# A cross-attention and expert kernel on one core: the gated bias in one product, the front's loads and clears laid out anew

## The reference, cut to what matters

```python
# x, ctx: (8, 256, 128)
n = layernorm(x)
q, k, v = heads(n @ W_Q.T), heads(ctx @ W_K.T), heads(ctx @ W_V.T)     # 8 heads of 16
attn = softmax(q @ k.T / 4, axis=heads)                                # over the heads
x = x + (attn @ v) @ W_O.T
n = layernorm(x)
logits = n @ Wr + br                                                   # 8 experts, best 2 kept
gates = softmax(where(top2, logits, -inf))
h = relu(n @ W1[e] + b1[e])                                            # 128 -> 256, each expert
x = x + sum_e gates[e] * (h @ W2[e]) + gates @ b2
```

## Time and profile before

| | |
|---|---|
| median of 3 runs | 209.75 us (209.21 to 209.9) |
| span of the profiled execution | 207.8 us, from its first instruction to its last |
| PE busy (matmuls) | 199.5 us, 96% |
| DVE / ACT / POOL busy | 167.8 / 132.2 / 112.3 us |
| instructions | 4986 |

### The profile page before, as it was taken

One profiled execution on the slowest core, in us unless ns is written; L12 is line 12 of the kernel. 1 busy time (PEld: TensorE's weight loads), 2 busy tenths in 40 slices (PEclk: granted clock), 3 DMA queues, 4 the chain that ended last, 5 costly groups with the idle time before them and its releaser, 6 DMA issues.

```text
span 207.8 us, 4986 instructions
## 1 busy us (share of the span) xinstructions
PE 199.5 (96%) x1752; PEld 176.5 (85%) x1752; DVE 167.8 (81%) x453; ACT 132.2 (64%) x316; POOL 112.3 (54%) x132
## 2 busy tenths in 40 slices
PE   6999988798999999999999999999999999999995
PEld 6845976686799979997999799998998899789994
DVE  6398769889789999899788988898999888556633
ACT  2236748697568847797677767677757776345441
POOL 8502647869976378629561966376746674010000
PEclk9999999999999999999999999999999999999999
DMA  6649595716515133423140504241000000000000
GB/s 175 160 127 286 153 279 148 224 46 183 158 62 145 69 108 106 103 76 104 41 147 25 170 3 151 57 144 36 0 0 28 0 2 3 25 3 2 25 3 25
DMA packets 20264, 18.70 MB, mean 90 GB/s; under 512 B 1776, under 2 KB 18704, under 8 KB 20240
## 3 DMA queue, kind: packets, MB, share of 16 engines
q1 hardware_dynamic: 17344, 16.85, 28.0%
q10 hardware_dynamic: 2896, 1.54, 2.8%
HBM read 11.83 MB, written 6.55 MB: 88 GB/s over the span
## 4 chain that ended last, share of the span: by engine, by line
PE 91%; DVE 3%; ACT 2%; issue 1%; POOL 1%; POOLq 0%; ACTq 0%; DVEq 0%
PE y_ps L436 28%; PE h_ps L421 22%; PE score_ps L361 7%; PE misc_ps L380 6%; PE score_ps L349 6%; PE h_ps L369 4%; PE score_ps L277 3%; PE misc_ps L401 2%; PE score_ps L338 2%; PE score_ps L421 2%; PE misc_ps L389 2%; PE misc_ps L287 1%; PE misc_ps L327 1%; PE misc_ps L306 1%; PE misc_ps L300 1%
## 5 line engine op out<-in xcount | busy, mean ns | idle before, releaser
L695 ACT ACTIVATE hT<-h_ps,b_sb 128x256 f32<-128x256 f32 x118 | 49.4, 470 | 33.3 <-PE h_ps L421 32.1
L436 PE MATMUL y_ps<-w_sb,hT 128*128 128x128 f32 x508 | 68.0, 277 | 0.0
L436 PEld LDWEIGHTS y_ps<-w_sb,hT 128*128 128x128 f32 x508 | 62.8, 191 | 3.5 <-issue 2.2
L1188 POOL TENSOR_TENSOR half_sum<-e_sb 128x512 f32<-128x512 f32 x28 | 37.3, 1332 | 30.8 <-ACT e_sb L667 30.5
L938 DVE TENSOR_TENSOR attn<-e_sb,e_rcp 128x1024 f32<-128x1024 f32 x32 | 42.1, 1319 | 3.3 <-ACT e_rcp L678 3.3
L930 DVE TENSOR_REDUCE shift_m<-score_ps 128x128 fp32r<-128x1024 f32 x32 | 38.7, 1212 | 2.2 <-PE score_ps L338 1.1
L421 PE MATMUL h_ps<-x1T_hi,w_lo 128*128 128x256 f32 x118 | 37.7, 320 | 1.5 <-ACT hT L695 0.9
L667 ACT ACTIVATE e_sb<-score_ps 128x1024 f32<-128x1024 f32 x32 | 32.8, 1024 | 5.6 <-PE score_ps L361 5.4
L1007 DVE SCALAR_TENSOR_TENSOR acc<-y_ps,gates,acc 128x128 f32<-128x128 f32 x96 | 29.0, 342 | 8.6 <-PE y_ps L436 7.3
L421 PE MATMUL h_ps<-x1T_hi,w_hi 128*128 128x256 f32 x118 | 33.1, 280 | 0.0
L421 PE MATMUL h_ps<-x1T_lo,w_hi 128*128 128x256 f32 x118 | 33.1, 280 | 0.0
(11 more groups left out here) (117 smaller groups left out, 291.3 us busy)
## 6 DMA issues: line engine op xcount, KB each, us to landing
k_scratch<-k_parts SPq DMA_DIRECT2D x14, 256.0 KB, 2.6
k_stack<-k_scratch SPq DMA_DIRECT2D x14, 256.0 KB, 4.0
q_stack<-q_scratch SPq DMA_DIRECT2D x28, 128.0 KB, 2.7
q_scratch<-q_parts SPq DMA_DIRECT2D x7, 256.0 KB, 2.7
w_sb<-in_w SPq DMA_DIRECT2D x1, 1024.0 KB, 6.6
out_y<-y_out SPq DMA_DIRECT2D x7, 128.0 KB, 1.9
x_all<-in_x ACTq DMA_DIRECT2D x1, 768.0 KB, 6.2
ctxT<-in_ctx_t SPq DMA_DIRECT2D x1, 640.0 KB, 6.1
```

The source lines that it names most:

```text
L436: mm = nc.tensor.matmul(product(j, t), hT[:, j % 2, c, t * P:(t + 1) * P], w2_sb[:, e * HC + c, :], start=(c == 0), stop=(c == HC - 1))
L695: op = nc.scalar.activation(hT[:, j % 2, c, :], hidden(j)[:, c * S:(c + 1) * S], ACT.Relu, bias=b1_sb[:, e * HC + c:e * HC + c + 1])
L1188: nc.gpsimd.tensor_tensor(half_sum[:], e[:, 0:HQ // 2], e[:, HQ // 2:HQ], ALU.add).then_inc(sum_step, 1)
```

## The change

It does these things; the orders on the engines are otherwise as before.

- The gated bias becomes two products of 128 x 128 weights by 128 columns in the rounded fp32r format. `b2_sb` is loaded as 16 stacked copies; `split_b2` on DVE makes from it the rows `b2_rows` (high part for most rows, low part for others). `transpose_gates` first writes the high part of the gates twice and their low part once into `gate_parts` (two more DVE instructions for each sample). `block_gates`, new on POOL, multiplies the transposed gates by `group_of`, so that `gatesD` is block diagonal. `gated_b2` now waits for `gates_blocked`, which POOL raises.
- `split_b2(0)` stands on DVE between `head_max(1, 1)` and `ln1(5 * TT, NT, 4)`; `block_gates(0)` and `block_gates(1)` on POOL behind `head_sum(2, 1)` and `head_sum(3, 1)`, and in `period` behind `head_sum(now, 1)`.
- The rows of sample 0 are loaded in two halves, first on each queue; the attention weights are second on ACT's queue; all other early loads go to SP's queue. b2 is one load in place of four, so the small loads count 64 and not 112.
- `neg_ident` is made by ACT. POOL's clears are cut in parts and stand behind `ln1_rstd_of` of sample 0 (`v_pad` of sample 0, gates, iota) and of sample 1 (the rest).
- `keep_warm(12)` is `keep_warm(8)`; the later `keep_warm` and both `fill` are gone.
- `expert_up(b, 0)` makes the four products with x1T_hi first and waits for x1T_lo only then.

```diff
             def gated_b2(b, freed, n):
                 if b == 0:
-                    pe.wait_ge(small_in, 112)
+                    pe.wait_ge(b2_rows_made, 1)
                 wait(pe, freed, n)
-                pe.wait_ge(gatesT_made, b + 1)
+                pe.wait_ge(gates_blocked, b + 1)
                 for t in range(TT):
-                    for g in range(P // 32):
-                        rows = slice(32 * g, 32 * g + E)
-                        mm = nc.tensor.matmul(misc_ps[32 * g:32 * g + 32, t * P:(t + 1) * P], gatesT[rows, t, :],
-                                              b2_sb[rows, :], start=True, stop=True)
+                    mm = nc.tensor.matmul(misc_ps[:, t * P:(t + 1) * P], gatesD[:, t, :, :].rearrange("p g k -> p (g k)"),
+                                          b2_rows[:], start=True, stop=True)
                 mm.then_inc(b2_done, 1)
...
                 if e == 0:
-                    pe.wait_ge(x1T_lo_made, b + 1)
+                    pe.wait_ge(x1T_hi_made, b + 1)
...
+                if e == 0:
+                    passes = [(c, w, x1T_hi) for c in range(HC) for w in (w1_lo, w1_hi)] + [(c, w1_hi, x1T_lo) for c in range(HC)]
...
+                    if e == 0 and k == 2 * HC:
+                        pe.wait_ge(x1T_lo_made, b + 1)
...
             def beginning():
                 project_k(0, None, 0)
                 project_v(0, None, 0)
-                keep_warm(5)
                 transpose_xn(0, None, 0)
-                keep_warm(1)
                 project_q(0, xnT_taken, 1)
                 project_k(1, k_first_made, 1)
-                keep_warm(2)
...
-                fill(4)
                 scores(1, 0)
...
-                fill(4)
                 transpose_x1n(0, v_taken, 3)
...
             def take_v(b):
                 wait(act, av_done, b - 3)
-                if b == 0:
-                    act.wait_ge(v_zeroed, 1)
+                if b < 4:
+                    act.wait_ge(v_zeroed, b + 1)
...
+            act.dma_start(x_all[:, 1, :], x_rows[:, 1, :]).then_inc(x0_in, 16)
             act.dma_start(w_qkvo[:], w_attn).then_inc(wq_in, 16)
             nc.scalar.preload_act_table_set("natural_log_exp_and_others")
...
+            act.wait_ge(ident_made, 1)
+            nc.scalar.activation(neg_ident[:], ident[:], ACT.Copy, scale=-1.0).then_inc(neg_ident_made, 1)
...
+            def split_b2(b):
+                dve.wait_ge(neg_ident_made, 1)
+                nc.vector.tensor_reduce(neg_lo_row[:], neg_ident[:].bitcast(F32).rearrange("p (g r) -> p g r", r=32)[:, :, 16:24],
+                                        AX.XY, ALU.min)
+                nc.vector.tensor_reduce(group_of[:], ident[:].rearrange("p (g r) -> p g r", r=32), AX.X,
+                                        ALU.max).then_inc(b2_step, 1)
+                dve.wait_ge(small_in, 64)
+                nc.vector.tensor_copy(b2_hi[:], b2_sb[:]).then_inc(b2_step, 1)
+                dve.wait_ge(b2_step, 2)
+                nc.vector.scalar_tensor_tensor(out=b2_rows[:], in0=b2_hi[:].bitcast(F32), scalar=neg_lo_row[:, 0:1], in1=b2_sb[:],
+                                               op0=ALU.mult, op1=ALU.add).then_inc(b2_rows_made, 1)
...
             def transpose_gates(b):
                 dve.wait_ge(gates_made, b + 1)
...
+                nc.vector.tensor_copy(gate_parts[:].rearrange("p t (k s) -> p t k s", s=2 * E)[:, :, :, 0:E],
+                                      gates[:, b % 2].unsqueeze(2).to_broadcast([P, TT, 2, E])).then_inc(gate_step, 1)
+                dve.wait_ge(gate_step, 2 * b + 1)
+                nc.vector.tensor_tensor(gate_parts[:, :, E:2 * E], gates[:, b % 2], gate_parts[:, :, 0:E].bitcast(F32),
+                                        ALU.subtract).then_inc(gate_step, 1)
...
+            def block_gates(b):
+                if b == 0:
+                    pool.wait_ge(b2_step, 1)
+                pool.wait_ge(gatesT_made, b + 1)
+                wait(pool, b2_done, b)
+                nc.gpsimd.tensor_tensor(gatesD[:], gatesT[:].unsqueeze(2).to_broadcast([P, TT, P // 32, 32]),
+                                        group_of[:].unsqueeze(1).unsqueeze(3).to_broadcast([P, TT, P // 32, 32]),
+                                        ALU.mult).then_inc(gates_blocked, 1)
...
             def beginning():
+                zero_v(0)
+                zero_gates()
+                iota8()
                 ln1_rstd_of(TT, 2 * TT, 1)
-                nc.gpsimd.memset(q_stack[:, 0].bitcast(F32), 0.0).then_inc(q_zeroed[0], 1)
+                zero_q(1)
+                zero_v(1)
+                zero_q(0)
+                zero_v(2)
+                zero_v(3)
                 ln1_rest(2 * TT, 3 * TT, 2)
...
                 head_sum(2, 1)
+                block_gates(0)
                 ln2_end(1)
```

More of the change, by code:

```diff
@@ L57, in build @@
         b2_sb = sb("b2_sb", [P, D])
+        b2_hi = sb("b2_hi", [P, D], F32R)
+        b2_rows = sb("b2_rows", [P, D], F32R)
+        neg_lo_row = sb("neg_lo_row", [P, 1])
+        group_of = sb("group_of", [P, P // 32])
         wr_sb = sb("wr_sb", [P, E])
@@ L112, in build @@
         gated_onehot = sb("gated_onehot", [P, 2, TT, E])
-        gates = sb("gates", [P, 2, TT, 32])
+        gates = sb("gates", [P, 2, TT, E])
+        gate_parts = sb("gate_parts", [P, TT, 32], F32R)
         gatesT = sb("gatesT", [P, TT, 32])
+        gatesD = sb("gatesD", [P, TT, P // 32, 32], F32R)
         hT = sb("hT", [P, 2, HC, S])
@@ L277, in keep_warm @@
                     nc.tensor.matmul(score_ps[:, 1, 0:P], ident[:], ident[:], start=True, stop=True, skip_group_check=True)
-            def fill(times):
-                pe.wait_ge(q_lo_made, 1)
-                for _ in range(times):
-                    nc.tensor.matmul(y_ps[:, 0, 0:P], ident[:], ident[:], start=True, stop=True, skip_group_check=True)
             def project_k(b, freed, n):
@@ L418, in expert_up @@
                     wait(pe, relu_made, j)
-                for c in range(HC):
-                    for k, (w, xt) in enumerate(((w1_lo, x1T_hi), (w1_hi, x1T_lo), (w1_hi, x1T_hi))):
-                        mm = nc.tensor.matmul(hidden(j)[:, c * S:(c + 1) * S], w[:, e, c * P:(c + 1) * P], xt[:, b % 2, :],
-                                              start=(k == 0), stop=(k == 2))
+                if e == 0:
+                    passes = [(c, w, x1T_hi) for c in range(HC) for w in (w1_lo, w1_hi)] + [(c, w1_hi, x1T_lo) for c in range(HC)]
+                else:
+                    passes = [(c, w, xt) for c in range(HC) for w, xt in ((w1_lo, x1T_hi), (w1_hi, x1T_lo), (w1_hi, x1T_hi))]
+                for k, (c, w, xt) in enumerate(passes):
+                    if e == 0 and k == 2 * HC:
+                        pe.wait_ge(x1T_lo_made, b + 1)
+                    mm = nc.tensor.matmul(hidden(j)[:, c * S:(c + 1) * S], w[:, e, c * P:(c + 1) * P], xt[:, b % 2, :],
+                                          start=(k == 0), stop=True, skip_group_check=True)
                 mm.then_inc(h_done, 1)
@@ L839, in beginning @@
                 relu(1, 5)
+            x_rows = x.rearrange("b (t p) d -> p (b t) d", p=P)
+            act.dma_start(x_all[:, 1, :], x_rows[:, 1, :]).then_inc(x0_in, 16)
             act.dma_start(w_qkvo[:], w_attn).then_inc(wq_in, 16)
             nc.scalar.preload_act_table_set("natural_log_exp_and_others")
[L843 to L852 removed]
+            act.wait_ge(ident_made, 1)
+            nc.scalar.activation(neg_ident[:], ident[:], ACT.Copy, scale=-1.0).then_inc(neg_ident_made, 1)
             beginning()
@@ L1096, in beginning @@
                 head_max(1, 1)
+                split_b2(0)
                 ln1(5 * TT, NT, 4)
@@ L1156, in _ @@
             dve.wait_ge(ident_made, 1)
-            nc.vector.tensor_scalar(neg_ident[:], ident[:], -1.0, None, ALU.mult).then_inc(neg_ident_made, 1)
             nc.vector.tensor_reduce(head_of[:], ident[:].rearrange("p (a o d) -> p o a d", o=H // 2, d=DH), AX.XY,
                                     ALU.max).then_inc(head_of_made, 1)
-            dve.wait_ge(x0_in, 16)
+            dve.wait_ge(x0_in, 32)
             ln1(0, TT, 0)
@@ L1202, in ln2_end, with zero_v, zero_q, zero_gates @@
                 nc.gpsimd.tensor_tensor(ln2_off[:], ln2_neg[:], ln2_rstd[:], ALU.mult).then_inc(ln2_off_made, 1)
+            def block_gates(b):
+                if b == 0:
+                    pool.wait_ge(b2_step, 1)
[4 more added lines that the diff above has]
+                                        ALU.mult).then_inc(gates_blocked, 1)
+            def zero_v(b):
+                nc.gpsimd.memset(v_pad[:, b], 0.0).then_inc(v_zeroed, 1)
+            def zero_q(slot):
+                nc.gpsimd.memset(q_stack[:, slot].bitcast(F32), 0.0).then_inc(q_zeroed[slot], 1)
+            def zero_gates():
+                nc.gpsimd.memset(gate_parts[:].bitcast(F32), 0.0).then_inc(gates_zeroed, 1)
+            def iota8():
```

(6 more changed lines are left out.)

44 lines of the change are left out of this document (20 added, 24 removed).

## The result

The changed kernel takes 219.92 us (median of 4 executions, 219.04 to 221.01) where the kernel before takes 209.75: a ratio of 1.049, 95% interval 1.046 to 1.053, so 4.9% slower. Its profiled execution has a span of 218.3 us, 10.5 more than before. I had forecast 210.9 with a range up to 215.7: the sign was right, the size was not.

A forecast was written before the change was run, and what follows sets the result against it. PE was taken as the bound from 39.46 us on, a chain through DVE, POOL and ACT just before. Terms -2.1 + 2.0 - 0.35 + 3.5 - 2.0 = +1.05 on span 207.8 gave 210.9 us, range 208.6 to 215.7.

The forecast's parts named there:

- The front: Loads and idle products before sample 0's first scores: `transpose_xn(0)` at 6.65, not 8.75, so 2.1 us gained.
- rival 1: POOL's clears hold DVE's second `ln1_end` (line 875) until 13.2: +4.4, 215.3 us; chance 0.27.
- the load of the stacked q: Failure sign: it might swallow the front's gain; the forecast had it moving along with the front.
- split_b2(0): Four DVE instructions ahead of `ln1` at 32.35, the cast meeting POOL's `half_sum`: +2.0 us, range 0.9 to 2.4.
- First expert product: First `expert_up` starts without `x1T_low`: 0.35 us saved once, between 0 and 0.44.
- The wait: PE at `gated_b2(0)` waits for POOL's `block_gates(0)`, once only: +3.5 us, bounds 3.3 to 4.3.
- rival 3: PE's clock falls at pauses near 25 us, before `transpose_x1n(0)` and at the first gated bias: 2.4 lost, 213.3 us; chance 0.12.
- DVE's instructions for the gates: Two small instructions ahead of the steady transpose, 0.45 us, within 0.76 of room: nothing lost.
- Seven cheaper biases: Gated bias on PE, samples 1 to 7, two products for sixteen records: 2.0 us saved, of 0.85 to 2.45.
- my case: The forecast's main case, all its terms summed: 210.9 us, own range 209.4 to 212.3; chance 0.46.

The follow-up runs named there:

- the profile with idle products: Changed kernel with 16 products of `ident` by `ident` ahead of PE's wait at `gated_b2(0)`: 217.20 us, 1.036.
- The bare wait: Kernel before with only one wait more, PE at `gated_b2` of sample 0 waiting for POOL's `head_sum(2, 1)`: 214.03 us, 1.020.
- four orders: Changed kernel with `block_gates(0)` and `split_b2(0)` earlier, clears behind DVE's second xn, steady `transpose_gates` behind `head_max(now, 2)`: 207.14 us, 0.987.
- the front alone: Changed kernel with the gated bias of before (sixteen products, no `split_b2`, no `block_gates`): 210.47 us, 1.002.

## Why the prediction was wrong

By its own steps, against the starts:

- **The front, -2.1.** Measured +0.6: the term that failed, and by 2.7. Two things were wrong in it. DVE's second xn was held by the clears: rival 1's mechanism, its price 2.7 and not my 4.4, since sample 0's xn was done at 5.58, not 6.1 to 6.6, and the clears ended at 12.13, not 13.2. And "all of what follows is a chain of unchanged steps" was wrong too: without the hold (clears alone moved) the first four exponentials gained 2.24, and the fifth lost it, to the stacked q and the clock. That the load of the stacked q swallows the gain I had named as what would make the prediction fail; I gave it no chance and no price.
- **split_b2(0), +2.0.** Measured +1.99. Place, partner (`half_sum`) and price right; the cast took 1.27 and the last of the four 0.83.
- **First expert product, -0.35.** Measured -0.12. The first relu is 0.44 earlier than the seventh exponential's shift; 0.12 of it is left at the tenth.
- **The wait, +3.5.** Measured 3.9 on PE, its releaser and its single occurrence right. Its cost was 6.7. What was missing is the clock, 2.95 by the profile with idle products. I had the fall of the clock as rival 3, at 2.4 us, as another case in place of mine. It wasn't another case: it is a consequence of the wait, and belonged into the sum with it. The bare wait in the kernel before shows the same (3.0 of wait, 4.6 of cost).
- **DVE's instructions for the gates, 0.** Failed. "Two small instructions ... 0.45 us ... 0.76 of room" took the duration from a row of a transpose that meets nothing. These meet `half_sum`: 1.29 for 16 elements in three steady periods, 1.21 for sample 1's cast. Sample 1 costs 0.95 by itself (+9.17 to +10.12), which my sum doesn't have.
- **Seven cheaper biases, -2.0.** PE's saving was 0.40 a sample, better than my 0.35, and the total was +0.4 in place of -2.0. The step that failed is the one above: in the changed kernel DVE is late for `subtract_max` three times, by up to 0.8. With the instructions moved and still held the steady gain is 0.12 a sample: PE then waits for DVE's `acc`, 0.13 in three periods and 0.41 in one, and its product there starts 0.3 later after `subtract_max` than in the kernel before. With them moved and not held (four orders) it is 0.48, and of these waits only the one of 0.41 is left, in the period where the subtraction took 1.15. My reason for taking 2.0 of 2.45, that "the saving brings PE up to DVE now and then", named the right engine; what made it late is the hold, which I had put at nothing.

+0.6 + 2.0 - 0.1 + 6.7 + 0.95 + 0.4 = 10.5, the difference of the spans. Against my +1.05 the misses are 2.7 (front), 3.2 (the clock mostly), 1.0 (sample 1) and 2.4 (steady). The range failed because I took the rivals to exclude each other: the clears and the clock both came, and their prices add. Even so my case with rivals 1 and 3 added is 217.7, 2.2 short of 219.92: DVE's instructions for the gates were in no rival.

Some of the prediction's arithmetic is off, by too little to matter here: 208.85 + 1.95 is 210.8, not 210.9; 32.35 to 34.9 is 2.55, not 2.4; and the ends of my own case's range are 209.8 and 212.05 by the terms named, not 209.4 and 212.3.

The Trainium skill, SBUF — State Buffer, section Who interferes with whom, has both holds: a `tensor_scalar` in a two-port mode against any GpSimd instruction, for which the trace now agrees at line 877 too (3.62 for 0.60), and a DVE instruction with two SBUF inputs against a GpSimd instruction that reads SBUF, for which it agrees at line 1005 (1.29 for 0.17), but for the three times in the kernel with four orders where both began within 4 ns and DVE took 0.17. I had weighed the first rule and gone against it for a form that the rows didn't settle, and not applied the second to `gates` minus `gate_parts`.

What stays open: why the clock falls behind some pauses and not behind others (2.53 us at 23.2 was followed by half speed, 2.30 at 24.2 in another kernel was not), why `block_gates(0)` moved alone once took only 210.79, what decides whether DVE's subtraction is held in its new place, and how much of the last 1.35 us is due to the idle products.

## What to carry to other kernels

A new wait on the bounding engine is priced with the clock behind it: look for what fills the pause, or add a slow stretch to the sum. A small DVE instruction is priced by its neighbour on POOL, not by its size: before adding one, list what POOL runs at that moment, whether it reads SBUF, and how many of the new one's inputs lie in SBUF; then put it where POOL is idle, or at least behind what the bounding engine waits for: that took the steady loss away here although the instruction was still held. Four changes of order, two on DVE and two on POOL, turned 4.9% slower into 1.3% faster, with the same arithmetic. Where several rivals have separate places in the program they are terms with a chance each, not alternatives, and the upper bound is their sum.

## What was new about the hardware

- A `tensor_scalar` whose two scalars come from memory is held by a row of POOL's clears like one with a constant: 3.62 us for 0.60, and not let in between five clears that follow each other; in one kernel of six with this row (the front alone) it ended at 11.29, ahead of the last two.
- A pause of PE of 3.0 to 3.9 us was followed by the clock's lower level for 3.4 and 6.8 us of uninterrupted work; in the profile with the pause of 3.9 filled with idle products it was not (2.9 us at the end). Pauses of 2.0 to 2.7 us were followed by it in some profiles and not in others.
- A DVE subtraction of 128 x 16 with both inputs in SBUF took 1.28 to 1.30 us where POOL's `half_sum` began 9 to 36 ns ahead of it, and 0.17 where it began 3 to 4 ns ahead; in the latter case `half_sum` itself took 1.33 in place of 1.28.
- Two fp32r products of 128 x 128 x 128 hold the chain for 0.17 us, where sixteen small full-precision ones held it for 0.57.
